# Order of VectorE's work in a batch of attention: division, root chain, scaling, maxima and input statistics moved

## What is computed

```python
h = _ln(x, ln1_g, ln1_b) + silu(t) @ W_ada.T + b_ada
qkv = (h @ Wqkv.T).reshape(b, n, 3, H, HD)
q, k = _ln(q, qn_g, qn_b), _ln(k, kn_g, kn_b)        # per head
attn = softmax(q @ k.T / sqrt(HD));  o = attn @ v
x = x + o @ Wout.T
gate = softmax(tok @ Wgate.T);  vals, idx = top_k(gate.T, 4096 // 8)
g = _ln(tok[idx], mlp_g, mlp_b)
tok[idx] += (gelu(g @ fc1.T + b1) @ fc2.T + b2) * vals
```

## Time and profile before

| | |
|---|---|
| runs, median (lowest to highest) | 1283.15 us (1282.36 to 1286.84), 3 runs |
| profiled execution, its time / span | 1289.48 us / 1287.7 us |
| TensorE busy | 1107.4 us, 86% |
| VectorE busy | 1049.3 us, 81% |
| ScalarE busy | 625.8 us, 49% |
| GpSimd busy | 564.7 us, 44% |
| mean granted TensorE clock | 0.945 |

### The profile page before, as it was taken

One profiled execution on the slowest core, in us unless ns is written; L12 is line 12 of the kernel. 1 busy time (PEld: TensorE's weight loads), 2 busy tenths in 40 slices (PEclk: granted clock), 3 DMA queues, 4 the chain that ended last, 5 costly groups with the idle time before them and its releaser, 6 DMA issues.

```text
span 1287.7 us, 24533 instructions
## 1 busy us (share of the span) xinstructions
PE 1107.4 (86%) x8291; PEld 854.8 (66%) x8291; DVE 1049.3 (81%) x1959; ACT 625.8 (49%) x1000; POOL 564.7 (44%) x507
## 2 busy tenths in 40 slices
PE   4689999999999999999999999999975036999996
PEld 3457676767767676767767676767754025898896
DVE  8688988888898988888888989888885884776773
ACT  4445555556465655555464655555440103444531
POOL 2465544444453544454454545454451202344333
PEclk9799999999999999999999999999997556999998
DMA  5000000000101000000001000000002203454322
GB/s 171 9 1 18 18 18 17 16 16 16 33 0 33 16 16 16 16 16 16 16 16 33 15 18 16 16 16 16 9 18 111 74 1 108 115 155 126 98 34 33
DMA packets 32277, 48.50 MB, mean 38 GB/s; under 512 B 7920, under 2 KB 28528, under 8 KB 30960
## 3 DMA queue, kind: packets, MB, share of 16 engines
q1 hardware_dynamic: 26096, 39.49, 9.4%
q0 software_dynamic: 6144, 8.52, 3.6%
HBM read 35.29 MB, written 12.71 MB: 37 GB/s over the span
## 4 chain that ended last, share of the span: by engine, by line
PE 62%; DVE 23%; issue 8%; POOL 3%; ACT 2%; DMA 2%; DVEq 0%; SPq 0%; ACTq 0%; POOLq 0%
PE ch L450 10%; PE ch L451 9%; PE ch L452 9%; PE av L1287 8%; PE sc L1312 7%; DVE rec L1140 4%; PE sc L1303 4%; PE av L1291 3%; PE pq L1265 3%; DVE qn L824 3%; PE mx L1323 2%; DVE var L1182 2%; POOL out L547 2%; DVE hit L704 1%; DVE oT L1142 1%
## 5 line engine op out<-in xcount | busy, mean ns | idle before, releaser
L916 POOL TENSOR_TENSOR qk_lo<-qkT,qk_hi 128x512 fp32r<-128x512 f32 x128 | 165.3, 1292 | 272.8 <-ACT qk_hi L982 272.8
L1140 DVE RECIPROCAL rec<-av 128x256 f32<-128x256 f32 x128 | 224.5, 1754 | 45.4 <-PE av L1291 44.9
L994 ACT ACTIVATE prob<-sc 128x1024 f32<-128x1024 f32 x128 | 131.5, 1027 | 237.5 <-PE sc L1312 237.5
L911 POOL TENSOR_TENSOR prob_sum<-prob 128x512 f32<-128x512 f32 x128 | 165.2, 1291 | 141.6 <-ACT prob L994 141.6
L450 PE MATMUL ch<-w_hi,hT_lo 128*128 128x512 f32 x384 | 174.0, 453 | 7.1 <-DVE w_lo L1062 7.0
L1287 PE MATMUL av<-prob,V 128*64 128x256 f32 x1024 | 141.0, 396 | 43.7 <-DVE oT L1142 41.6
L1162 DVE TENSOR_REDUCE m<-mx 128x4 bf16<-128x1024 f32 x128 | 155.4, 1214 | 0.0
L451 PE MATMUL ch<-w_lo,hT_hi 128*128 128x512 f32 x384 | 153.8, 401 | 0.0
L452 PE MATMUL ch<-w_hi,hT_hi 128*128 128x512 f32 x384 | 152.9, 398 | 0.0
L1287 PEld LDWEIGHTS av<-prob,V 128*64 128x64 f32 x1024 | 65.6, 137 | 101.4 <-issue 81.3
L1098 DVE TENSOR_REDUCE ssum<-sq 128x8 f32<-128x512 f32 x128 | 84.8, 680 | 55.2 <-ACT sq L961 53.4
(11 more groups left out here) (195 smaller groups left out, 2760.2 us busy)
## 6 DMA issues: line engine op xcount, KB each, us to landing
fcw<-experts SPq DMA_DIRECT2D x8, 2048.0 KB
x_sb<-x SPq DMA_DIRECT2D x16, 256.0 KB, 2.7
xr_sb<-x SPq DMA_DIRECT2D x16, 256.0 KB, 2.8
out<-tok SPq DMA_DIRECT2D x16, 256.0 KB, 2.2
rows_dram<-xh SPq DMA_DIRECT2D x16, 256.0 KB, 2.2
prob<-w_qkvT SPq DMA_DIRECT2D x2, 512.0 KB, 7.9
qn<-w_qkvT SPq DMA_DIRECT2D x2, 512.0 KB, 8.5
V<-w_qkvT SPq DMA_DIRECT2D x2, 512.0 KB, 8.2
```

The costliest lines, as they stand in the source:

```text
L911: nc.gpsimd.tensor_tensor(prob_sum[(hp - 1) % 2][:, :, :], pr[:, :, 0, :], pr[:, :, 1, :], ALU.add).then_inc(prob_summed, 1)
L916: nc.gpsimd.tensor_tensor(qk_lo[par][:, :], qkT[par][:, :], qk_hi[par][:, :].bitcast(F32), ALU.subtract).then_inc(lo_ready, 1)
L994: nc.scalar.activation(prob[hp % 2][:, :], sc[:, :], ACT.Exp, scale=HD ** -0.5).then_inc(prob_ready, 1)
L1140: chain(nc.vector.reciprocal(rec[:, :], av[:, N:2 * N]))
```

## The change

In VectorE's `batch`:

- the root chains move one slot on, from the end of slots 0 and 4 to slots 1 and 5, between the division and the maxima (`inverse_roots`);
- the scaling of a group moves from slots 1 and 5 to slots 2 and 6, behind the maxima, on VectorE and on GpSimd; `xh2` follows it from slot 5 to slot 6, behind it;
- in slots 0, 3, 4 and 7 the maxima stand between the two sums of squares;
- the statistics of x move from slot 0 to slot 3 and are those of batch b+2, their roots come from the chain in slot 5, and `xh` moves from slot 1 to slot 6. x of batch 0 is treated ahead of the first call.

SP's load of x goes with it (batch b+2 in place of b+1). The loop runs over batches 2 to 13, and 14 is unrolled. TensorE's and ScalarE's programs keep their order.

```diff
-FIRST_LOOPED, LAST_LOOPED = 2, B - 2
+FIRST_LOOPED, LAST_LOOPED = 2, B - 3
...
+def has_second(b):
+    return not isinstance(b, int) or b + 2 < B
...
+    batch(B - 2, cur=True, nxt=True, prv=True)
...
-                if nxt and not (isinstance(b, int) and b < 0):
-                    need(xh_ready, b + 1)
+                if has_second(b):
+                    need(xh_ready, b + 2)
...
-                    if hp == 1 and cur:
+                    if hp == 2 and cur:
                         normalise(0, 0)
-                    if hp == 5 and nxt:
+                    if hp == 6 and nxt:
                         normalise(4, 0)
...
+            def inverse_roots(b, hp, nxt):
+                if hp == 0 or nxt:
+                    need(chunk_summed, through("chunk", b, (hp, 1)))
+                    ins = nc.vector.tensor_scalar(var[:, 0:NH], ssum[:, :], 1.0 / HD, EPS, ALU.mult, ALU.add)
+                    if hp == 0:
+                        chain(ins)
+                if hp == 4:
+                    chain(nc.vector.tensor_scalar(var[:, NH:NH + 4], mv[:, :, 1], EPS, None, ALU.add))
+                need(qn_pool_ready, b * 2 + (0 if hp == 0 else 1))
+                rsqrt(chain, NH if hp == 0 else NH + 4, rstd[1 if hp == 0 else 0])
...
-                    if hp == 1 and nxt:
-                        need(rstd_ready, through("newton", b, 0))
...
                         nc.vector.tensor_copy(o_hi[:, (hp - 1) % UNITS, :], o[:, :]).then_inc(normed, 1)
-                    if hp == 0 and nxt:
-                        need(x_in, (b + 2) * 16)
+                    if (hp == 1 and cur) or (hp == 5 and (nxt or prv) and not last_entry):
+                        inverse_roots(b, hp - 1, nxt)
+                    if hp == 3 and has_second(b):
+                        need(x_in, (b + 3) * 16)
                         row_stats(x_sb, 0)
                     if hp in (0, 3, 4, 7) and (cur if hp < 2 else nxt):
                         head_sums(b, hp, 0)
-                        head_sums(b, hp, 1)
...
                                                 AX.X, ALU.max).then_inc(max_ready, 1)
-                    if hp == 5 and prv and not last_entry:
-                        token_rows(b)
-                    if (hp == 1 and cur) or (hp == 5 and nxt):
+                    if hp in (0, 3, 4, 7) and (cur if hp < 2 else nxt):
+                        head_sums(b, hp, 1)
+                    if (hp == 2 and cur) or (hp == 6 and nxt):
...
                         for c in range(POOL_CHUNKS, 4):
-                            ins = times_rstd(nc.vector, 1 if hp == 1 else 0, c)
+                            ins = times_rstd(nc.vector, 1 if hp == 2 else 0, c)
                         ins.then_inc(qn_ready, 1)
+                    if hp == 6 and prv and not last_entry:
+                        token_rows(b)
+                    if hp == 6 and has_second(b):
+                        need(rstd_ready, through("newton", b, 4))
+                        need(slot_filled, through("slot", b if cur else -1, (1, 2)))
+                        input_rows(rstd[0])
...
-                    if (hp == 0 and (cur or nxt)) or (hp == 4 and (nxt or prv) and not last_entry):
...
```

More of the change, by code:

```diff
@@ L95, in make_counts @@
                 hit("chunk", b, key)
-        for hp, live in ((0, cur or nxt), (4, nxt or prv)):
+        for hp, live in ((0, cur or b < 0), (4, nxt or prv)):
             if live:
@@ L830, in batch @@
             def batch(b, cur, nxt, prv):
-                if nxt and not (isinstance(b, int) and b < 0):
-                    need(xh_ready, b + 1)
-                    sp.dma_start(x_sb[:, :, :], x[bass.ds(b + 1, 1)].rearrange("o (t p) d -> p (o t) d", p=P)
-                                 if not isinstance(b, int) else x[b + 1].rearrange("(t p) d -> p t d", p=P)).then_inc(x_in, 16)
+                if has_second(b):
+                    need(xh_ready, b + 2)
+                    sp.dma_start(x_sb[:, :, :], x[bass.ds(b + 2, 1)].rearrange("o (t p) d -> p (o t) d", p=P)
+                                 if not isinstance(b, int) else x[b + 2].rearrange("(t p) d -> p t d", p=P)).then_inc(x_in, 16)
                 if prv:
@@ L1084, in token_rows, with input_rows @@
                 ins.then_inc(xh2_ready, 1)
+            def input_rows(factors):
+                for t in range(TT):
+                    ins = nc.vector.tensor_scalar(xh[:, t, :], x_sb[:, t, :], mv[:, t, 0:1],
+                                                  factors[:, NH + t:NH + t + 1], ALU.subtract, ALU.mult)
+                ins.then_inc(xh_ready, 1)
+            def inverse_roots(b, hp, nxt):
[8 more added lines that the diff above has]
+                rsqrt(chain, NH if hp == 0 else NH + 4, rstd[1 if hp == 0 else 0])
             def last_rows():
@@ L1099, in head_sums @@
                                         sq[c % 2][:, :].rearrange("p (h d) -> p h d", d=HD), AX.X, ALU.add).then_inc(chunk_summed, 1)
+            need(x_in, 16)
+            row_stats(x_sb, 0)
+            chain(nc.vector.tensor_scalar(var[:, NH:NH + 2], mv[:, 0:2, 1], EPS, None, ALU.add))
+            rsqrt(chain, NH + 2, rstd[1])
+            need(rstd_ready, 1)
+            input_rows(rstd[1])
             def batch(b, cur, nxt, prv):
@@ L1163, in batch @@
                                                 AX.X, ALU.max).then_inc(max_ready, 1)
-                    if hp == 5 and prv and not last_entry:
-                        token_rows(b)
-                    if (hp == 1 and cur) or (hp == 5 and nxt):
-                        g = b * 2 + (1 if hp == 1 else 2)
-                        need(rstd_ready, through("newton", b, hp - 1))
+                    if hp in (0, 3, 4, 7) and (cur if hp < 2 else nxt):
+                        head_sums(b, hp, 1)
+                    if (hp == 2 and cur) or (hp == 6 and nxt):
+                        g = b * 2 + (1 if hp == 2 else 2)
+                        need(rstd_ready, through("newton", b, hp - 2))
                         need(qk_transposed, (g - 1) * GU)
                         for c in range(POOL_CHUNKS, 4):
-                            ins = times_rstd(nc.vector, 1 if hp == 1 else 0, c)
+                            ins = times_rstd(nc.vector, 1 if hp == 2 else 0, c)
                         ins.then_inc(qn_ready, 1)
+                    if hp == 6 and prv and not last_entry:
[4 more added lines that the diff above has]
+                        input_rows(rstd[0])
                     if hp == 2 and prv and not last_entry:
@@ L1177, in batch @@
                         row_stats(tok, 2)
-                    if (hp == 0 and (cur or nxt)) or (hp == 4 and (nxt or prv) and not last_entry):
[L1180 to L1194, removed]
+            per = 35
             def counted(b, cur, nxt, prv):
```

## The result

The changed kernel takes 1533.56 us (median of 4 runs, 1530.29 to 1539.98), against 1284.45 us for the kernel before in 4 runs: a ratio of 1.1945, 95% interval 1.1898 to 1.1992. It is 249 us slower; 209 were forecast, and 1492 us with a range of 1400 to 1540. The time lies near the upper end of that range.

The account below looks back on a forecast made before the run. The kernel was taken as nearly bound by TensorE (62% of the chain of waits, VectorE 23%). 146 + 69 − 6.5 + 1 = +209 us on 1283 gave 1492 us, range 1400 to 1540.

Parts of the forecast that it names:

- signs named: L1265 waits 31 times, some 5.5 us in slot 3 and 3 in slot 7; batch period 71 to 73 us.
- Step 1: Slots 1 and 2: chain behind slot 1's division costs 2.9 to 4.0 us; scores 1.1 to 2.2 us late.
- Step 2: Scaling in slot 2: ends 8.6 us after the maximum's start; TensorE's slot 3 begins 7.1 us late.
- Step 3: Slot 3: clock loss after TensorE's wait, 2.5 us; slots 0 to 3 cost 9.1 us, 16 times, +146 us.
- Step 4: Slots 5 to 7: slot 7 begins 2.6 us later, plus 2.0 for the clock; 15 times, +69 us.
- rival of more collisions: A second GpSimd operation meets each chain and the clock costs 3.4 and 2.7 us: 1571 us, chance 0.11.
- Step 5: The rest: moved statistics and xh hidden, second sums 0; batch 0 gives back 6.5 us, prologue costs 1.
- Full clock: Same waits in slots 0 to 3 and 5 to 7, clock stays at 2.4 GHz: 1422 us, chance 0.20.
- Faster: Slot 5's division no longer waits behind the chain and nothing replaces that wait: 1240 us, chance 0.04.
- The rule weighed: VectorE and GpSimd hold the shared port pair for whole instructions; both moved chains pay a collision: about 1512 us.

Follow-up runs that it names:

- e2: Kernel before with input statistics, their roots and xh half a batch ahead, and the scaling and xh2 one slot later; chains unmoved: 1487.74 us.
- e3: Changed kernel with VectorE's scaling back in slots 1 and 5, GpSimd's chunk behind its sum of exponentials in slots 2 and 6: 1385.72 us.
- e4: Changed kernel with 19, 10, 6 and 11 unused filler matmuls ahead of TensorE's waits in slots 3, 7, 2 and 6: 1451.92 us.
- e7: Changed kernel with one Newton step in place of three in each chain: 1428.22 us.
- e5: Changed kernel with both chains moved behind the maxima of slots 1 and 5: 1481.69 us.
- e1: Changed kernel with the order of the kernel before; only input statistics, their roots and xh stay half a batch ahead: 1295.54 us.
- e9: Kernel before with only the maxima of slots 0, 3, 4 and 7 put between the two sums of squares: 1265.0 us.
- e8: Kernel before with the second chain in slot 5 behind the maxima, xh2 and GpSimd's scaling chunk in slot 6: 1308.01 us.
- e10: Kernel before with the maxima between the sums of squares in slots 0, 3, 4, 7, and slot 5's scaling ahead of xh2: 1281.81 us.

## Why the prediction was right, point by point

**What bounds it.** Right: the bound was the wait of L1265 (L1279 after) for the scaling, 32 times, 147 us (138 without the 9.1 of the prologue); forecast were 31 waits of 5.5 and 3 us, 133 us. VectorE stands idle 4.10 us ahead of `tok`; 4 were forecast. The rule that the slack of 1.67 us would not bear a slot's shift holds by e2 and e3. The sum came out 40 us low: slots 0 to 3 were forecast at 146 us and took 142, slots 5 to 7 at 69 and took 112, and batch 0 and the prologue gave back 10 for 5.5. So of the signs named, the waits came as listed, but the period is over the 71 to 73 us.

**Step 1** (2.9 to 4.0 us, scores of slot 2 late by 1.1 to 2.2): 3.64 us from 647.81 to 651.45 with one collision (`var_half` 1.11 us); TensorE waited 1.86 us ahead of the scores.

**Step 2** (8.6 us from the maxima to the end of the scaling): from 651.45 to 660.05, 8.6. Slot 3 came 7.57 us late against 7.1. The high part met nothing, as the 0.3 us end had it, but the split of hT did, 0.92 and 1.11 us for 0.42 and 0.69.

**Step 3** (2.5 us for the clock in slot 3): too high. It was 1.4 us in the batch shown (4.77 us where 549.37 to 552.78 in the kernel before is 3.41), and 1.8 on average (5.28 against 3.45 in e4). The waits of slots 0 to 3, read in e4 at full clock, cost 7.0 us for the 6.6 forecast. The two errors are of opposite sign, and that 8.9 us stand against 9.1 is partly luck.

**Step 4** was the term that was mis-sized: +2.6 us for slots 5 to 7 and 2.0 for the clock, 69 us in all; it measured +5.5 and +2.0 on average, 112 us (5.55 and 2.37 in the batch shown). In e4, at full clock, the same slots are 3.6 us longer than before, and that is the waits, for 2.6. The other 3.9 are clock, for 2.0: 2.3 behind slot 7's start, near the 2.0, and 1.5 ahead of it, which the forecast did not have. Two readings explain what was missing. "The chain ... takes from 3.13 us ... to the 4.45": it took 5.05, as the last two of its eleven instructions ran into GpSimd's next two operations (1.15 and 0.65 us for 0.20 each); the rival of more collisions had priced that at 1.1 us, and it was 0.6. "About 0.5 us waiting for the gate logits": 1.98, since the 3.25 us wait ahead of the scores of slot 6 let the clock fall and the scores and the gate product ran at 1.2 GHz (their first step takes 1.01 us for 0.60), on the path to the maxima and to the scaling. The clock was put only behind the last wait, and it acted between two as well. e7 shows both in reverse, and e5 the second.

**Step 5.** "Hidden: the first by VectorE's wait for the attention product of slot 3" holds in the changed kernel, where VectorE was idle 4.04 us there, but only because TensorE is late; in e1, without that cover, it cost 11 us, 0.8 us a batch, near the 0.7 that the step named as its price. "Second sums behind the maxima ... 0" was wrong: the maxima themselves wait for nobody, but the chain behind them does; e9 shows 1.8%. In the changed kernel the chain is no longer there and the gain with it.

**The rivals.** Full clock (1422): the clock did fall, and e4, which holds it at 2.4 GHz, shows that the waits alone cost more than that rival had, 7.0 and 3.6 us a batch for 6.6 and 2.6; it takes 1452. More collisions (1571) was half right in slots 5 to 7. Faster: the 2.21 us wait did go, and 3.25 us came in the same slot.

**The rule weighed.** That VectorE and GpSimd exclude each other on the shared port for an instruction (the Trainium skill, SBUF — State Buffer, the section on its two sides) put the forecast at 1512, nearer to the 1534 than mine. The rows agree for small instructions: `var_half` of 0.18 us takes 1.05 to 1.11. For long ones they nearly do: in e8 the scaling takes 3.81 us, where VectorE's 1.88 and GpSimd's 1.04 and 1.27 one after the other would be 4.19. But the rule did not find the term that was missing most, the clock between two waits.

## What to carry over

Where an in-order consumer opens a stage with a wait for a late result, measure the slack between that result's end and the stage's start, and move nothing past it that is longer: here 1.67 us against a scaling that ended 9.2 us later (1.67 + 7.57). Look for a neighbour's idle time first: exchanging the maxima with one sum that had to wait anyway gave 1.8%, where moving whole steps lost 19%. After a reorder, read what each instruction now lies beside, GpSimd's work above all, and the clock behind a wait, not only what it follows.

## Not expected of the hardware

Two neighbouring VectorE steps exchanged cost 17 us of 1265, and the rows that got longer are those that lie beside GpSimd's work (e9, e10). Filling idle TensorE time pays: 46 matmuls a batch of no use brought back 5.5 us (82 us in fifteen batches), as the work behind the waits no longer ran at 1.2 GHz. And e8 waits no longer than the kernel before (2.9 against 3.1 us a batch), but its 2.42 us wait ahead of slot 7 is followed by 1.2 GHz in every batch, where the 2.21 us wait in slot 6 left the clock at 1.00 in thirteen of fifteen windows. Why one does and the other does not is not shown.
